# A graph attention and relation layer: selectors and one-hots of two steps per ScalarE activation

## What is computed

```python
# layer 0, h = relu(layernorm(x))
Q = (h @ Wq).reshape(n, H, HD); K, V = the same with Wk, Wv
score = einsum('ehd,ehd->eh', Q[dst], K[src]) / sqrt(HD)
score = score + relu(efeat @ W1 + b1) @ W2 + b2
ex    = exp(score - segment_max(score, dst)[dst])
alpha = ex / segment_sum(ex, dst)[dst]
out   = segment_sum(alpha[:, :, None] * V[src], dst) @ Wo + bo
x = x + out
# layer 1: per-relation messages, gated, summed by dst, relu, added to x
```

## Time and profile before

| | us |
|---|---|
| median of 2 runs | 5446.34 (5445.96 to 5446.73) |
| the profiled execution | 5449.73 |
| its span in the trace | 5447.9 |
| fused stage, main part, from the trace | about 240 to 2630 |
| PE busy over the span | 4660.0 (86%) |
| DVE / ACT / POOL busy over the span | 3301.0 / 3291.8 / 3285.8 |

### The profile page before, as it was taken

The page is one execution under the profiler, slowest core; times in us unless marked ns, Lnnn a source line. Parts: engine busy times, 40 slices in busy tenths (PEclk is TensorE's granted clock), DMA queues, the critical chain, the costliest instruction groups (busy, mean ns, idle before and its releaser), DMA issues. The chain is left out here.

```text
span 5447.9 us, 89819 instructions
## 1 busy us (share of the span) xinstructions
PE 4660.0 (86%) x20748; PEld 2699.6 (50%) x20749; DVE 3301.0 (61%) x7106; ACT 3291.8 (60%) x7926; POOL 3285.8 (60%) x3364
## 2 busy tenths in 40 slices
PE   8799999999999999998899999777777777676766
PEld 5455555555555555555444444344444444444443
DVE  6489999999999999999633333333333333333334
ACT  3489999898999999897544444333333333333333
POOL 0277777777777777777200000477777777777776
PEclk9899999999999999999899999866666666767777
DMA  4588888888888888887434344333333333333334
GB/s 139 161 242 239 238 241 241 238 240 239 240 241 241 242 238 239 236 240 230 146 140 142 139 142 141 124 105 105 105 105 105 105 105 105 105 105 105 105 105 141
DMA packets 542017, 932.63 MB, mean 171 GB/s; under 512 B 102705, under 2 KB 351631, under 8 KB 541712
## 3 DMA queue, kind: packets, MB, share of 16 engines
q0 software_dynamic: 208384, 648.75, 41.3%
q1 hardware_dynamic: 333328, 280.23, 15.9%
HBM read 795.82 MB, written 132.87 MB: 170 GB/s over the span
## 5 line engine op out<-in xcount | busy, mean ns | idle before, releaser
L1033 POOL DMA_INDIRECT kv_rows<-kv_d,idx x1664 | 1695.7, 1019 | 671.4 <-issue 380.7
L1813 PE MATMUL m_sums<-m_rows,m_oh 128*128 x3328 | 1389.5, 566 | 590.3 <-ACT m_rows L1793 517.3
L1750 POOL DMA_INDIRECT m_rows<-msg_d,m_idx x1568 | 1487.4, 949 | 507.2 <-issue 472.7
L1793 ACT ACTIVATE m_rows<-m_rows,m_norm 128x256 f32<-128x256 f32 x1568 | 710.8, 500 | 1267.5 <-DMA m_rows<-msg_d,m_idx 1267.5
L1813 PEld LDWEIGHTS m_sums<-m_rows,m_oh 128*128 128x128 f32 x3328 | 836.1, 275 | 1143.8 <-issue 1021.2
L1835 DVE TENSOR_TENSOR agg<-agg,m_sums 128x256 f32 x832 | 350.2, 421 | 1297.1 <-PE m_sums L1813 1293.7
L1227 PE MATMUL sums<-kv_rows,onehot 128*128 128x264 f32 x3328 | 942.2, 406 | 17.9 <-issue 10.0
L1227 PEld LDWEIGHTS sums<-kv_rows,onehot 128*128 128x128 f32 x3328 | 570.3, 191 | 398.4 <-issue 226.0
L1683 PE MATMUL p_m<-wr,h1T 128*128 128x512 f32 x1568 | 711.1, 597 | 0.0
L1184 PE MATMUL p_q<-shelf,pickT 128*128 x4992 | 696.1, 275 | 12.2 <-ACT pickT L1090 9.5
L1067 ACT ACTIVATE hid<-p_hid,b1s 128x512 f32<-128x512 f32 x784 | 494.3, 682 | 194.2 <-PE p_hid L1164 193.1
(11 more groups left out here) (194 smaller groups left out, 3903.0 us busy)
## 6 DMA issues: line engine op xcount, KB each, us to landing
msg_d<-msg SPq DMA_DIRECT2D x196, 512.0 KB, 2.9
dsts<-dstrow_d SPq DMA_DIRECT2D x208, 256.0 KB
ef_raw<-in_edge_attr_dram SPq DMA_DIRECT2D x195, 256.0 KB
kv_rows<-kv_d,idx POOLq DMA_INDIRECT x1664, 3.9
m_rows<-msg_d,m_idx POOLq DMA_INDIRECT x1568, 2.7
kv_d<-kvo SPq DMA_DIRECT2D x49, 260.0 KB, 2.1
pens<-pens_d SPq DMA_DIRECT2D x52, 192.5 KB
emlp<-mlp_d SPq DMA_DIRECT2D x52, 128.0 KB
```

Source lines behind the costliest of these rows:

```text
L1033: pool.indirect_dma_start(rows[:, lane, k, a:a + KV], None, kv_d[:, :], bass.IndirectOffsetOnAxis(idx[:, half, c:c + 1], 0)).then_inc(gath ...
L1750: pool.indirect_dma_start(rows[:, u, k, :], None, msg_d[:, :], bass.IndirectOffsetOnAxis(idx[:, u // HALF, c:c + 1], 0)).then_inc(gathered ...
L1793: last = nc.scalar.activation(rows[:, u, k, :], rows[:, u, k, :], ACT.Copy, scale=norm[:, bass.ds(2 * g + k, 1)])
L1813: last = nc.tensor.matmul(sums[u % BANKS][:, 0:D], onehot[:, u % HOTS, k, :], rows[:, bass.ds(slot, 1), k, :].rearrange("p a d -> p (a d)" ...
```

## The change

ACT makes selectors and one-hots for two steps with one activation each. `far_node`, `pickT` and `onehot` activations grow from 256 to 512 elements per partition and their number halves; `far_dst` stays at one activation per 128 elements, four in a row instead of two. Selectors are made in slots 0 and 2, for steps s+2 and s+3, both activations behind the slot's MLP piece. One-hots are made in slots 1 and 3, for steps s-19 and s-18. There are four one-hot places instead of two, and the semaphores count pairs. PE and DVE keep their instructions and order; PE's select and add_up wait for the pair that holds their step, and SP's load of `dsts` for the pair count.

```diff
-HOTS2 = 2
+HOTS2 = 4
@@ SP, load_dsts
-                    sp.wait_ge(pick_ready, U * (m - 1))
+                    sp.wait_ge(pick_ready, U * (m - 1) // 2)
@@ ACT
-            def measure(s, x, u, n):
-                if u == 0:
-                    act.wait_ge(dsts_in[x], 16 * (n + 1))
-                if not first(s):
-                    act.wait_ge(pick_ready, s)
-                nc.scalar.activation(far_node[:, :], dsts[:, x, u, :], ACT.Abs, scale=-1.0, bias=t["node"][:, 0:1]).then_inc(far_ready, 1)
-
-            def pick(s, u):
-                act.wait_ge(far_ready, s + 1)
-                if not (isinstance(s, int) and s < PICKS):
-                    act.wait_ge(q_done, s + 1 - PICKS)
-                nc.scalar.activation(pickT[:, u, :], far_node[:, :], ACT.Relu, scale=-1.0,
+            def select_pair(s):
+                m, u, n = s // U, s % U, s // 2
                 if u == 0:
+                    act.wait_ge(dsts_in[m % 2], 16 * (m // 2 + 1))
+                wait(act, pick_ready, n)
+                nc.scalar.activation(far_node[:, :, :], dsts[:, m % 2, u:u + 2, :], ACT.Abs, scale=-1.0,
+                                     bias=t["node"][:, 0:1]).then_inc(far_ready, 1)
+                act.wait_ge(far_ready, n + 1)
+                wait(act, q_done, s + 2 - PICKS)
+                nc.scalar.activation(pickT[:, s % PICKS:s % PICKS + 2, :], far_node[:, :, :], ACT.Relu, scale=-1.0,
                                      bias=t["one"][:, 0:1]).then_inc(pick_ready, 1)
@@ ACT, body
-                    if is_step(s + 3):
-                        measure(s + 3, (u + 3) // U % 2, (u + 3) % U, QUADS // 2 * i + (u + 3) // (2 * U))
-                    if is_step(s - LATE):
+                    if u % 2 == 1 and is_step(s - LATE):
                         measure_dst(s - LATE)
                     if is_quad(m + 1):
                         ...
-                    if is_step(s + 3):
-                        pick(s + 3, (u + 3) % PICKS)
-                    if is_step(s - LATE):
-                        hot(s - LATE, (u - LATE) % HOTS2)
+                    if u % 2 == 0 and is_step(s + 2):
+                        select_pair(s + 2)
+                    if u % 2 == 1 and is_step(s - LATE):
+                        hot(s - LATE)
@@ PE
             def select(s, u, b):
-                pe.wait_ge(pick_ready, s + 1)
+                pe.wait_ge(pick_ready, s // 2 + 1)
             def add_up(s, u, c):
-                pe.wait_ge(hot_ready, s + 1)
+                pe.wait_ge(hot_ready, s // 2 + 1)
```

More of the change, by code:

```diff
@@ L822, in attend @@
         dsts = sb("dsts", [P, 2, U, 2 * P], BF16)
-        far_node = sb("far_node", [P, 2 * P], BF16)
+        far_node = sb("far_node", [P, 2, 2 * P], BF16)
         pickT = sb("pickT", [P, PICKS, 2 * P], BF16)
-        far_dst = sb("far_dst", [P, 2, P])
+        far_dst = sb("far_dst", [P, 4, P])
         onehot = sb("onehot", [P, HOTS2, 2, P])
@@ L1091, in pick @@
+                act.wait_ge(far_ready, n + 1)
+                wait(act, q_done, s + 2 - PICKS)
+                nc.scalar.activation(pickT[:, s % PICKS:s % PICKS + 2, :], far_node[:, :, :], ACT.Relu, scale=-1.0,
                                      bias=t["one"][:, 0:1]).then_inc(pick_ready, 1)
             def measure_dst(s):
-                if not first(s):
-                    act.wait_ge(hot_ready, s)
-                for k in range(2):
+                wait(act, hot_ready, s // 2)
+                for k in range(4):
@@ L1097, in measure_dst @@
                     nc.scalar.activation(far_dst[:, k, :], t["iota"][:, :], ACT.Abs, scale=-1.0,
[L1098 to L1105, removed]
+                                         bias=t["dst"][:, 2 * s + k:2 * s + k + 1]).then_inc(fard_ready, 1)
@@ L1107, in weights, with hot @@
+            def hot(s):
+                act.wait_ge(fard_ready, 2 * s + 4)
+                wait(act, summed, s + 2 - HOTS2)
+                nc.scalar.activation(onehot[:, s % HOTS2:s % HOTS2 + 2, :, :].rearrange("p s k n -> p (s k) n"), far_dst[:, :, :],
+                                     ACT.Relu, scale=-1.0, bias=t["one"][:, 0:1]).then_inc(hot_ready, 1)
             def weights(c, x):
@@ L1133, in body @@
                         take_ef(m + 2)
-                    if is_step(s + 3):
-                        pick(s + 3, (u + 3) % PICKS)
-                    if is_step(s - LATE):
-                        hot(s - LATE, (u - LATE) % HOTS2)
+                    if u % 2 == 0 and is_step(s + 2):
+                        select_pair(s + 2)
+                    if u % 2 == 1 and is_step(s - LATE):
+                        hot(s - LATE)
                     if u % R == 3 and is_chunk(c):
                         weights(c, (u // R - 1) % 2)
-            for s in range(3):
-                measure(s, 0, s, 0)
-                pick(s, s)
+            select_pair(0)
             act.wait_ge(w_in, WIN)
```

## The result

| | before | after |
|---|---|---|
| median, us | 5446.34 | 5873.61 (5872.21 to 5875.02) |
| ratio, 95% interval | | 1.078 (1.076 to 1.080) |
| span of the profiled execution, us | 5447.9 | 5873.2 |
| ACT busy over the span, us | 3291.8 | 3126.6 |
| a step of the fused stage (2000 us by DVE's additions), us | 2.915 | 3.442 |

A forecast was written before the change was run, and what follows sets the result against it. PE sets the pace, DVE for 1.61 us a chunk; ACT waits. Stalls of 2.00 and 0.82 us a quad make 11.28 us a chunk, less 1.61 hidden, times 49: 474 us, about 5920 us (range 5760 to 6010).

The forecast's parts named there:

- the sum: Fused stage: 49 chunks, each longer by a net 9.67 us, make 474 us of loss.
- ACT isn't the bound, and its saving is worth nothing: ACT in the fused stage: some 0.9 us saved per two steps gains nothing, since ACT waits for PE at `hid`.
- The stall of slot 0, 2.00 us: PE's select after slot 0's sums: selectors come at 3.83 us, weight load is due at 1.83, so PE stands 2.00 us.
- the walk: Slot 0, from PE's `hidden` through ACT's `hid`, far_node and pickT: selectors reach PE after 3.83 us.
- The stall of slot 2, 0.82 us: PE's select after slot 2's sums: pair comes 2.56 us after `mlp_out` starts, wanted at 1.74, so PE stands 0.82 us.
- What the stalls hide, 1.61 us a chunk: Chunk's first quad: PE's waits for DVE's `top`, `fall` and `fwd`, 1.61 us a chunk, fall away behind the new stalls.
- The first quads, counted like all others: Start of the stage: all 196 MLP quads, 49 chunks, were given the same loss, 9.67 us a chunk.
- The one-hots, `dsts`, `efT` and DVE cost nothing: Fused stage: paired one-hots, the `dsts` load and `efT` come in time, and DVE is no bound; cost nothing.
- The clock rival: PE's idle pieces lower its clock; a mean loss of a tenth adds 244 us, about 6160 us; chance 0.07.
- the forecast of 1.00: Sign of a right forecast: PE's clock stays at 1.00 in the fused stage; below that would favour the clock rival.

The follow-up runs named there:

- the kernel with the pair ahead: Changed kernel with the 512-wide selector pair (far_node, pickT) moved ahead of ACT's MLP piece in slots 0 and 2: 5445.5 us, ratio 0.9997 to the kernel before.
- the two singles: Changed kernel with each selector pair made, in the same place, as two 256-wide selectors with a count each: 5736.2 us, ratio 1.051 to the kernel before.
- Abs ahead: Changed kernel with the pair's far_node (Abs) ahead of ACT's MLP piece and only pickT (Relu) behind: 5629.2 us, ratio 1.033 to the kernel before.

## Why the prediction was right

5920 us were predicted, with a range of 5760 to 6010; 5874 came, 427 us of loss where the sum had 474. The mechanism and both stalls were as forecast. That the sum came within 47 us is in part luck, since four sizes were off and two pulled against the others: -41 us at the stalls, -41 at what they hide, +31 from the clock, +8 in the first quads, which leaves 4.

- **ACT isn't the bound, and its saving is worth nothing.** Right: the kernel with the pair ahead has the saving and not the stalls, and takes the time of the kernel before. The saving itself was put too high: 0.9 us per two steps were forecast, 165/416 = 0.40 came. The forecast added up durations, but activations overlap: in the kernel before, `onehot` starts at 1206.79, 0.40 us after a `pickT` that lasts 0.51. Nothing in the sum hung on it.
- **The stall of slot 0, 2.00 us.** Measured 1.91. The activations took 0.72 us where I had 0.70, and the gap inside the pair was 0.03 where I had 0.05, so the selectors were there at 3.80, close to the walk. The term that was off is PE's: from pickT's end to the weight load went 0.15 us, not 0.05, but from weight load to first matmul only 0.01, where the earlier trace rows have 0.22 for a select that comes behind running matmuls. I counted the stall at the weight load, where it was 3.95 - 1.83 = 2.12 us, and so missed the 0.21 us that PE wins back when it has stood.
- **The stall of slot 2, 0.82 us.** Measured 0.74, for the same reason. A quad grew by 13.18 - 10.57 = 2.61 us, not 2.82: 0.21 x 4 x 49 = 41 us too many in the sum.
- **What the stalls hide, 1.61 us a chunk.** Measured 4 x 2.61 - 7.99 = 2.45, at a clock of 1.00. The listed waits for `top`, `fall` and `fwd` did vanish, and part of the other 2.8 us of the chunk's first quad with them. That is 0.84 x 49 = 41 us more hidden.
- **The first quads, counted like all others.** They lost more. Without sums between `hidden` and the select nothing covers the pair: a quad took 261.31 - 247.80 = 13.51 us, where it took 9.69 before. The first `score` came at 288.4 us instead of 272.4, 16 us later, where a chunk at a clock of 1.00 loses 8.

```profile
247.80 1.13 PE L1155 MATMUL p_hid<-efT,w1s 64*128 64x512 f32 x4
251.76 1.28 PE L1175 MATMUL p_q<-shelf,pickT 128*128 x6 [2.83 <-ACT pickT L1087]
...
261.31 1.13 PE L1155 MATMUL p_hid<-efT,w1s 64*128 64x512 f32 x4
```

In the kernel before (timeline of PE, two `hidden` of slot 0 that follow each other):

```profile
243.50 1.13 PE L1164 MATMUL p_hid<-efT,w1s 64*128 64x512 f32 x4
...
253.19 1.13 PE L1164 MATMUL p_hid<-efT,w1s 64*128 64x512 f32 x4
```

- **The one-hots, `dsts`, `efT` and DVE cost nothing.** Right for the changed kernel; `efT` was the next to be late, as the two singles showed.
- **The clock rival.** At its price of a tenth it did not come: 0.99 over 2000 us. But the forecast of 1.00 was not met either, and the 31 us that the clock cost were in no term. Some of the gaps did bring it down, as here, with `hidden` at 2.08 us instead of 1.13, and the window around it:

```profile
2902.84 0.93 PE L1175 MATMUL p_q<-shelf,pickT 128*128 x6 [1.74 <-ACT pickT L1087]
...
2904.29 2.08 PE L1155 MATMUL p_hid<-efT,w1s 64*128 64x512 f32 x4
```

```profile
2902.00:2908.00 6.00, 5.16 (x23) 2.51 (x24) 2.55 (x5) 3.44 (x8) 3.83 (x4) 0.72 0.62 170
```

## What to carry to other kernels

Before one activation is made to serve two steps, note for the first of the two who wants it and when, and what stands ahead of it on its own engine: a busy share of 90% did not make ACT the bound, and 165 us of saved work cost 427 us because the pair came one slot nearer to its use, behind a wait. If an engine waits for another's work of the same slot, put everything that this other engine will want next ahead of that wait, or one slot earlier; either takes two lines and undid the loss whole. A walk from the release to the use with the trace's start-to-start distances gave the stalls to 0.1 us; what they hide elsewhere, and what they do to the clock, was the less certain half.

## What the runs showed of the hardware

**POOL's weighing holds up a DVE operation with two SBUF operands beside it, even one on eight numbers.** `newmax`, on 1 x 8 numbers, went from a median of 0.16 to 1.76 us, `place` from 0.34 to 1.32 (its mean 1.23), and `top` has 1.27 us beside POOL and 0.69 apart from it. All three take both operands from SBUF. The Trainium skill, "SBUF — State Buffer", section "SBUF: two separate sides", says that DVE and GpSimd share a pair of ports as an exclusive lock for a whole instruction, and that a DVE operation with two SBUF inputs falls under it against a GpSimd operation that reads SBUF. These rows agree; the operation's own length doesn't enter. One thing is left open: `newmax` is held for 1.60 us, longer than the weighing's 1.09, and its row starts 0.64 us ahead of the weighing's. Nothing here shows what holds it in that time.

**The clock after gaps of the same length differs.** After most of the idle times of 1.74 us on PE the clock stayed at 2.4 GHz, after that at 2902.84 it was at 1.2 for some us. Where PE's longest idle time between 400 and 2400 us was shorter, 0.99 us with Abs ahead and 1.32 with the two singles, the clock was 1.00 throughout.
